# A 1024-deep matmul stage in seven chained products, and shorter eigenvector stages, in a two-layer graph kernel

## The reference, cut to what matters

```python
# layer 0
h = relu(layernorm(x))
w = adj * adj
h = relu(w @ (h @ W1))      # W1 256 x 512
h = relu(w @ (h @ W2))      # W2 512 x 1024
x = x + w @ (h @ W3)        # W3 1024 x 256
# layer 1
h = relu(layernorm(x))
deg = adj.sum(0) + adj.sum(1) - diag(adj)
L = D^-1/2 (diag(deg) - adj) D^-1/2
_, U = eigh(L)              # reads one triangle, 256 x 256
h = relu((U.T @ h) @ V1 + b1)   # V1 256 x 128
x = x + U @ (h @ V2 + b2)       # V2 128 x 256
```

## Time and profile before

| | us |
|---|---|
| median of three runs | 2317.81 |
| the profiled execution | 2316.99 |
| its span, first to last instruction | 2315.3 |
| busy in it: TensorE | 2287.5 |
| VectorE | 2000.3 |
| ScalarE | 1060.2 |
| POOL | 782.5 |

### The profile page before, as it was taken

The page is one execution under the profiler, slowest core; times in us unless marked ns, Lnnn a source line. Parts: engine busy times, 40 slices in busy tenths (PEclk is TensorE's granted clock), DMA queues, the critical chain, the costliest instruction groups (busy, mean ns, idle before and its releaser), DMA issues.

```text
span 2315.3 us, 42683 instructions
## 1 busy us (share of the span) xinstructions
PE 2287.5 (99%) x11050; PEld 1883.7 (81%) x11050; DVE 2000.3 (86%) x10266; ACT 1060.2 (46%) x2517; POOL 782.5 (34%) x1524
## 2 busy tenths in 40 slices
PE   7999999999999999999999999999999999999999
PEld 5777888887777788887777788888888888889998
DVE  7999999999999888878888889699999997457776
ACT  5444455554444444444444434344444444245554
POOL 5223333333232333333333353223333333133332
PEclk9999999999999999999999999999999999999999
DMA  2000000000000000000000000000000001024443
GB/s 103 28 28 28 19 19 28 28 28 28 19 28 28 28 19 19 28 27 28 28 28 28 19 28 28 28 10 28 27 27 27 28 28 37 19 66 130 135 133 108
DMA packets 90015, 89.93 MB, mean 39 GB/s; under 512 B 5376, under 2 KB 89088, under 8 KB 89856
## 3 DMA queue, kind: packets, MB, share of 16 engines
q1 hardware_dynamic: 89856, 88.23, 11.8%
HBM read 54.66 MB, written 33.55 MB: 38 GB/s over the span
## 4 chain that ended last, share of the span: by engine, by line
PE 63%; DVE 33%; ACT 2%; issue 2%; POOL 0%; DVEq 0%; POOLq 0%
PE ps L1473 47%; PE ps L1652 10%; DVE ps L1082 6%; DVE ahead L1085 3%; PE ps L1383 3%; DVE shared L1166 3%; DVE ps L1163 2%; DVE A L885 2%; DVE ahead L1061 2%; DVE A L889 1%; PE ps L1662 1%; DVE negs L1088 1%; ACT squares L614 1%; DVE xrow_sb L894 1%; PE ps L1599 1%
## 5 line engine op out<-in xcount | busy, mean ns | idle before, releaser
L1473 PE MATMUL ps<-w,hid2T 128*128 128x256 f32 x2048 | 466.0, 379 | 0.3 <-ACT hid2T L674 0.3
L1473 PEld LDWEIGHTS ps<-w,hid2T 128*128 128x128 f32 x2048 | 379.9, 190 | 50.4 <-issue 0.5
L468 POOL COPY Eb<-sc 128x1 f32<-128x1 f32 (+1 forms) x254 | 47.1, 185 | 700.2 <-DVE v L910 387.1
L1473 PE MATMUL ps<-agg2T,w 128*128 128x256 f32 x1024 | 240.0, 379 | 0.0
L1473 PE MATMUL ps<-hid2T,xin 128*128 128x256 f32 x1024 | 236.1, 379 | 0.8 <-ACT h2T L667 0.8
L1473 PE MATMUL ps<-weightT,hid 128*128 128x256 f32 x1024 | 235.6, 379 | 0.0
L1473 PE MATMUL ps<-w,aggT 128*128 128x512 f32 x512 | 231.8, 592 | 0.0
L1473 PEld LDWEIGHTS ps<-weightT,hid 128*128 128x128 f32 x1024 | 190.1, 191 | 35.3 <-issue 13.1
L1082 DVE RECIPROCAL ps<-ahead 128x40 f32<-128x40 f32 (+1 forms) x768 | 217.9, 329 | 0.1
L1473 PEld LDWEIGHTS ps<-hid2T,xin 128*128 128x128 f32 x1024 | 189.3, 190 | 25.6 <-ACT h2T L667 1.2
L1473 PEld LDWEIGHTS ps<-agg2T,w 128*128 128x128 f32 x1024 | 189.5, 190 | 24.7
(11 more groups left out here) (364 smaller groups left out, 5274.4 us busy)
## 6 DMA issues: line engine op xcount, KB each, us to landing
xl<-in_x_dram SPq DMA_DIRECT2D x64, 256.0 KB, 2.8
xr<-in_x_dram SPq DMA_DIRECT2D x64, 256.0 KB, 2.8
x_dram<-xr SPq DMA_DIRECT2D x64, 256.0 KB, 2.3
xin<-x_dram SPq DMA_DIRECT2D x64, 256.0 KB, 2.8
out_dram<-xin SPq DMA_DIRECT2D x64, 256.0 KB, 2.1
w<-in_L_gnn_W_dram SPq DMA_DIRECT2D x1, 2048.0 KB, 11.3
w<-in_L_gnn_W_dram SPq DMA_DIRECT2D x1, 1024.0 KB, 12.3
w<-in_L_gnn_W_dram SPq DMA_DIRECT2D x1, 512.0 KB, 6.7
```

The lines of the kernel that those rows point to most:

```text
L468: pool.tensor_copy(Eb[:, bass.ds(k, 1)], sc[:, 4:5])
L1473: ins = pe.matmul(dst, a, b, start=start, stop=stop, skip_group_check=stage[0] == "P")
```

## The change

Four things change, and the tables of the order with them.

*The 1024-deep stage.* `g3` becomes seven products G1 to G7, one for each 128 x 128 block position of the result, 14 units of four 128x128 matmuls. Their stationary tiles are blocks of the relu'd hidden features, or sums of them, which POOL makes in eight new operations a pair of 128x512 each (`LEFTS`); the moving ones are blocks of W3, or their sums, made once. Three additions of 128x256 (`G3_ADDS`) join the products. The `agg` units of the next pair now stand between P4 and G1.

*The Sturm stage.* After the count at 16 points there are three rounds of 7 points (14 columns) instead of two of 20 (40 columns).

*T and the signs.* POOL builds T in five operations once the tridiagonal matrix is known, where VectorE had ten; operands of the tree of signs lie in PSUM; Z is scaled and turned right behind the root, ahead of the differences of the eigenvalues; the first statistics of layer 1 move up into the first correction.

*The order.* Eleven pairs of 11 steps, ten of 12 and one of 13: 22 pairs with steps beside. The counts' transposes move into the second pair alone, ahead of its unit 34. A pair has 40 units, the last 38. The parts of the refinement have new places.

```diff
-KS = 20
-ROUNDS = 2
+KS = 7
+ROUNDS = 3
...
+        T, R, E, winv = A, prods, below, V
...
-        GROUPS = [(n, n + 1, 11, 0.54) for n in range(8)]
-        GROUPS += [(8, 10, 12, 0.54), (10, 11, 12, 0.54), (11, 12, 13, 0.54), (12, 16, 12, 0.54), (16, 20, 14, 0.54),
-                   (20, 21, 13, 0.54)]
+        GROUPS = [(n, n + 1, 11, 0.54) for n in range(11)]
+        GROUPS += [(11, 12, 12, 0.54), (12, 21, 12, 0.54), (21, 22, 13, 0.54)]
...
-        REFINE_AT, TURN_AT, VECTORS_AT = (24, 26, 29, 33, 35, 38, 42), 62, 65
+        COUNTS_AT, REFLECTORS_AT = 34, 3
+        REFINE_AT, TURN_AT, VECTORS_AT = (10, 13, 19, 23, 28, 34, 41), 60, 62
...
+            units = [("hid", j, q) for j in range(2) for q in range(NB)]
+            units += [("agg2", j, q) for q in range(H1B // 2) for j in range(2)]
+            units += [(p, half, 0) for p in ("P1", "P5", "P6", "P3", "P7", "P2", "P4") for half in range(2)]
+            units += [("agg", j, 0) for j in range(2)] * next_agg
+            units += [(p, m, 0) for p in ("G1", "G2", "G6", "G5", "G7", "G3", "G4") for m in range(NB)]
+            units += [("res", j, 0) for j in range(2)]
...
+                if part == 1:
+                    pool.wait_ge(fin, len(FINS) * pair + 3 + half)
+                    ins = pool.tensor_tensor(left_sum(1, half), c12, c22, ALU.add)
+                elif part == 2:
+                    pool.wait_ge(fin, len(FINS) * pair + 5 + half)
+                    pool.wait_ge(left_ready, len(LEFTS) * pair + 1 + half)
+                    ins = pool.tensor_tensor(left_sum(2, half), left_sum(1, half), c11, ALU.subtract)
+                elif part == 3:
+                    pool.wait_ge(fin, len(FINS) * pair + 5 + half)
+                    ins = pool.tensor_tensor(left_sum(3, half), c11, c12, ALU.subtract)
+                else:
+                    pool.wait_ge(evac, before(pair) + FULL.at["P4", half, 0] + 3)
+                    pool.wait_ge(left_ready, len(LEFTS) * pair + 3 + half)
+                    ins = pool.tensor_tensor(left_sum(4, half), c21, left_sum(2, half), ALU.subtract)
+                ins.then_inc(left_ready, 1)
...
+            pool.wait_ge(tri_v, 1)
+            all_of = lambda t, n: t.unsqueeze(1).to_broadcast([P, NB, n])
+            pool.tensor_tensor(T[:, :, :], ident[:, :, :], all_of(Db[:, :], N), ALU.mult).then_inc(t_built, 1)
...
+            dve.wait_ge(t_built, 5)
             link(dve.tensor_tensor(Zsq[:, :, :], Z[:, :, :], Z[:, :, :], ALU.mult))
             dve.tensor_reduce(nrm[:, 0, :], Zsq[:, :, :], AX.X, ALU.add).then_inc(z_root_in, 1)
...
-            link(ins)
-
-
-
-            for b in range(NB):
-                link(dve.tensor_tensor(T[:, b, :], ident[:, b, :], Db[:, :], ALU.mult))
...
+            ins.then_inc(z_ready, 1)
+
+            dve.wait_ge(z_turned, 1)
+            dve.tensor_copy(flat(Zt), ps[0][:, :]).then_inc(zt_ready, 1)
             dve.wait_ge(lam_top, 1)
...
-                if stage == "g3":
-                    order = (0, 1, 4, 5, 2, 3, 6, 7) if seven_ else range(H2B)
-                    return sum([group(half[m], [(hid2T[:, j, d, P * m:P * m + P], w3[:, d, :]) for d in order])
-                                for m in range(NB)], [])
...
+                if stage[0] == "G":
...
+                    return [(bank[:, 0:P], left(h_)[:, d, P * j:P * j + P], right(h_)[:, d, :],
+                             "P" + stage[1] not in ONTO and (h_, d) == (0, 0), (h_, d) == (1, 1))
+                            for h_ in range(2) for d in range(2)]
...
+                if (stage, j) == ("G1", 0):
+                    pe.wait_ge(fin, len(FINS) * pair + len(FINS))
+                if (stage, j) == ("G2", 0):
+                    pe.wait_ge(evac, before(pair) + plan_.at["P4", 1, 0] + 3)
+                if stage in ("G6", "G7", "G3") and j == 0:
+                    pe.wait_ge(sums_ready, 2 * len(S_TURNS))
+                    pe.wait_ge(left_ready, len(LEFTS) * pair + {"G6": 4, "G7": 6, "G3": 8}[stage])
+                if (stage, j) == ("res", 0):
+                    pe.wait_ge(g3_added, len(G3_ADDS) * pair + len(G3_ADDS))
...
-            for n in range(2 * len(FRAGS7)):
+            for n in range(PERIOD + len(ENDING.units)):
```

More of the change, by code:

```diff
@@ L244, in gnn_spectral_kernel @@
[L244 to L251, removed]
-        PRODUCTS = [(p, half) for p in ("P1", "P5", "P6", "P3", "P7", "P2", "P4") for half in range(2)]
-        UNITS7 = [("agg", j, 0) for j in range(2)] + [("hid", j, q) for j in range(2) for q in range(NB)]
@@ L266, in seven, with plan @@
[L266 to L272, removed]
-        def beside(steps, share, work):
+        Plan = namedtuple("Plan", "units at")
+        def plan(next_agg):
+            units = [("hid", j, q) for j in range(2) for q in range(NB)]
[4 more added lines that the diff above has]
+            units += [("res", j, 0) for j in range(2)]
+            return Plan(units, {n: i for i, n in enumerate(units)})
@@ L276, in beside, with before @@
+        FULL, ENDING = plan(1), plan(0)
+        PERIOD = len(FULL.units)
+        FIRST_P = FULL.at["P1", 0, 0]
+        SIZE = {"hid": 4, "G1": 1, "G2": 1, "G3": 1, "G4": 1, "G5": 1, "G6": 1, "G7": 1}
+        WORK = [(i, m, SIZE.get(st, 2)) for i, (st, _, _) in enumerate(FULL.units) for m in range(2 if st == "hid" else 4)]
+        def before(pair):
+            return PERIOD * pair + 2
+        def beside(steps, share):
             filled = [([], []) for _ in range(steps)]
-            total, done = sum(size for _, _, size in work), 0
@@ L278, in beside @@
-            for i, m, size in work:
+            total, done = sum(size for _, _, size in WORK), 0
+            for i, m, size in WORK:
                 step, place = divmod(done * steps / total, 1)
@@ L331, in placed @@
+        def placed(steps, share):
+            filled = beside(steps, share)
+            tau = 62.0 / steps
+            first, last, size = {}, {}, collections.Counter()
             for s, slot in enumerate(filled):
@@ new lines, in placed @@
+            free = dict.fromkeys(("pe", "pool", "act"), 0.0)
+            began, ended, slots = {}, {}, {}
+            while any(lines.values()):
+                ready = []
+                for line, events in lines.items():
+                    if events and all(x in ended for x in needs(*events[0])):
+                        engine = "act" if line in ("evac", "fin") else line
+                        start = max([free[engine]] + [ended[x] + 0.1 for x in needs(*events[0])])
+                        ready.append((start, line != "fin", line, engine))
+                start, _, line, engine = min(ready)
+                kind, n = event = lines[line].pop(0)
+                took = {"unit": size[n] * 62.0 / total if kind == "unit" else 0, "g3": 0.75, "fin": 0.65,
+                        "evac": 0.35 if kind == "evac" and FULL.units[n][0][0] == "G" else 0.65}.get(kind, 1.35)
+                began[event], ended[event] = start, start + took
+                free[engine] = start + took
+                behind = [slots[x] for x in needs(kind, n) if x in slots]
+                if kind == "unit":
+                    assert all(x <= first[n] for x in behind), (event, steps)
+                    slots[event] = last[n]
+                elif kind == "evac":
+                    slots[event] = last[n]
+                else:
+                    wanted = int((start + 0.4) // tau) if kind == "fin" else int(max(start - 3.2, 0) // tau)
+                    slots[event] = max(behind + [min(wanted, steps - 1)])
```

640 lines of the change are left out of this document (322 added, 318 removed).

## The result

The changed kernel takes 2333.55 us (median of four runs, 2333.07 to 2334.30), the kernel before 2317.88 in the same comparison: a ratio of 1.0066 (95% interval 1.0053 to 1.0079), slower by 15.7 us. The forecast was 2324 in a range of 2284 to 2342. The profiled execution took 2334.30, its span 2332.6.

The account below looks back on a forecast made before the run. Two equally long chains, TensorE's pairs and VectorE's Sturm and scan work, were taken to bound the kernel until 1940 us, TensorE alone afterwards. Span 2315.3 + 30 (D) - 25.8 (Z) + 3.2 (R), plus 1.7 outside: 2324 us, range 2284 to 2342.

Parts of the forecast that it names:

- two chains of one length: From the last Householder step to 1940 us, TensorE's pairs and VectorE's Sturm and scan work run side by side, meeting within a microsecond.
- A pair: One pair on TensorE without steps beside it: falls by 1.32 us to 57.34, its new 1024-deep stage taking 12.5.
- D: Time to the end of the last Householder step: +30 us, between +24 and +38, putting it at 1392.8.
- perhaps two more such steps in each early pair (+3): Householder steps: POOL's eleven new additions a pair delay VectorE's L919, 0.22 us free and 0.70 beside a POOL addition; +3 us.
- Z: From the last Householder step to the eigenvectors' readiness on VectorE: 577.6 us falls by 25.8 to 551.8.
- the 88.7: A 14-column Sturm round before added waiting: 88 us by the slope of older rounds plus 0.7 for an index comparison.
- The scans: VectorE's scans and sums behind the recurrence meet POOL more often: +2.4 us.
- The count wait: VectorE's wait before L1125 for the counts' transposes ends 114.6 us after the last Householder step instead of 122.4: -7.8.
- R: From the eigenvectors' readiness to the end: +3 us, bounds 0 and +8, including 2 for a slower clock after TensorE's wait.
- TensorE as the bound: Whole run: TensorE stays the limit, so 42.3 us and some idle time go; 2272 us, chance 0.12.
- POOL costs it nothing more: VectorE is the bound without added cost from POOL, rounds of 85 us and smaller growth before them; 2292 us, chance 0.18.
- POOL as the bound of the deep stage: 1024-deep stage: POOL's stretched differences make G3 and res wait about 1 us in 22 pairs; 2346 us, chance 0.10.

Follow-up runs that it names:

- the kernel with both edits: Changed kernel with 21 instead of 22 pairs beside the steps and L996 as two 128x1 instructions: 2285.99 us, ratio 0.9861 to the kernel before.

## Why the prediction was right or wrong

**The bounds of before.** Right: "two chains of one length". Shortening VectorE's alone by 33 us moved the time by 2 to 3.

**A pair.** Right: seven products from 1771.04 to 1783.55 in a pair alone, 12.51 us (forecast 12.5), and a pair of 57.4 (57.34):

```profile
1771.04 3.73 PE L1532 MATMUL ps<-w,hid2T 128*128 128x128 f32 x32
...
1783.55 3.62 PE L1532 MATMUL ps<-g,weightT 128*128 128x256 f32 x16
```

**D.** Wrong by 23.3 us, the largest miss. Its work was right: from the first pair's start (12.6) to the last step TensorE is busy 1372.7 us, before 1340.5, which is 32.2 more (forecast 33.1). The idle time was not: 30.8 against 9.7, so 21 us more instead of 3 less. The step that failed is "perhaps two more such steps in each early pair (+3)". There were two more held steps a pair, but each cost 1.05 us instead of 0.48, and the old ones grew to the same. The 0.70 of the earlier trace rows was read as the price of a hold; it was the rest of a POOL operation that happened to have begun 0.60 us ahead:

```profile
191.63 1.28 POOL L521 TENSOR_TENSOR hid2T<-backT,hid2T 128x512 f32<-128x512 f32 x1 [2.14 <-ACT hid2T L667]
```

In all these rows the price is what is left of POOL's instruction, up to all of its 1.27 us, and so it depends on which operation POOL has queued behind the save. Without holds the last step is at 1385.7, 7 below the forecast.

**Z.** Wrong by 13.8 the other way, in two terms. The rounds took 90.2 instead of 93: contention was as forecast (9 us of holds on L1139, which went with the points in PSUM, and 3 on the sign product L1166: 4 a round), but the free round is 86, not 88.7. The forecast counted the holds twice: the 88.7 was drawn through rounds that had them already. In the first count of before, 92.9 us, the sixteen L1061 have a mean of 546 ns where a free one takes 0.41 us, and with the product of the signs some 3.6 us are holds; in the two wide rounds they are some 5 and 10. Less these, the same slope gives about 86 for 14 columns. The row is of VectorE's groups from 1373 to 1462, before:

```profile
L1061 DVE TENSOR_TENSOR ahead<-Db,points 128x256 f32<-128x256 f32 x16 | 8.1, 546 | 0.0
```

The scans took 3.6 us less instead of 2.4 more: I had POOL meet them more often, while TensorE's own wait, which the same text forecasts, leaves POOL without work there. The count wait was right within 0.1 us (D + 114.5).

**TensorE's wait and R.** TensorE is there at D + 503 (forecast 501); it waits 36 instead of 51, by the two misses of Z and the 2 us it comes later. R is right. The clock was at its lower level (1.2 GHz) behind the rest of 35.9 us: the first 4 us read 0.50 granted, the first 7.8 us together 0.74, and from there on it is 1.00:

```profile
1955.20:1963.00 7.80, 7.77 (x29) 6.72 (x30) 6.38 (x9) 3.85 (x14) 0.41 (x3) 0.74 0.00 0
```

The 24 records behind the turn took 6.72 + 0.17 us instead of 5.2 + 0.17, and the turn itself 1.12 instead of 0.60 as before: 2 us.

**The rivals.** TensorE as the bound (2272) did not come; it needs the two instructions of one element and the 21 pairs, and even then the best is 2284. "POOL costs it nothing more" (2292) was wrong in its premise. POOL as the bound of the deep stage did not come: no wait for it stands in TensorE's list. That the time came within 10 us of the forecast is partly luck: D missed by 23.3 one way and Z by 13.8 the other.

**Who holds whom.** The Trainium skill, "SBUF — State Buffer", section "Who interferes with whom", names a second case that I left out: `tensor_scalar` from SBUF to SBUF may run in a mode that takes the shared ports whole. The runs agree in what they touch, but for the two short leads above: the 128x2 form is held (L996); the 128x1 form never is; the form that writes PSUM is not (with the order swapped, 33 of them began under a long POOL operation and took 0.22); an instruction with two SBUF inputs is (L1139, and in the kernel with both edits L1257); with one of them in PSUM it is not. I had cited the rule for L1061 and priced L919 from a row.

## What to carry to other kernels

A short instruction at a fixed place of a chain can meet another engine's long one at every pass, because the chain itself releases that engine: look for a group whose mean moved without its shape, and at who starts just ahead of it. Once seen, it costs little to avoid: here two instructions of one element gave 29 us, 0.13 us of order 21, and PSUM for an operand of the rounds 6. When a change makes the other chain the longer one, look at how much work stands ahead of that chain's result: one pair fewer there gave 18 us. The same stage was worth nothing where VectorE set the end, and likely some 30 us where TensorE did; both figures are argued.

## What was not expected of the hardware

An instruction of two elements a lane took 1.26 us against 0.22 free when it began 0.03 us behind a POOL operation of 1.27, and 0.23 when it began 0.10 ahead; the POOL operation's length showed no difference. At 0.03 and 0.06 ahead it still took 1.32 and 1.35. Two instructions of one element each at the same place took 0.33 together and were not held in 254 cases. VectorE's two-input instructions of 510 and 512 columns took 1.6 to 1.7 us beside a busy POOL and 0.69 alone, so a rest of TensorE gave VectorE's scans 7 to 10 us back.
